# A split float32r down projection and a norm formed in the layer before it

## The reference

```python
y = depthwise7x7(x) ; y = layernorm(y) * ln_w + ln_b
y = gelu(y @ w1 + b1)                              # 192 -> 768 channels
gx = sqrt(sum(y**2, axis=(1, 2), keepdims=True))   # per image and channel
nx = gx / (mean(gx, axis=-1, keepdims=True) + 1e-6)
y = grn_gamma * (y * nx) + grn_beta + y
out = x + (y @ w2 + b2)                            # 768 -> 192 channels
```

## Time and profile before

| | |
|---|---|
| median of 3 runs (lowest to highest) | 3556.2 us (3555.02 to 3557.4) |
| the profiled execution: its own time | 3558.36 us |
| its span, first to last instruction | 3556.6 us |
| mean granted TensorE clock | 0.979 |
| TensorE, VectorE, ScalarE, GpSimd busy | 96%, 67%, 50%, 30% |
| down projection, first to last product | 2793.96 to 3178.3 us |
| the norm's block | 2779.1 to 2790.9 us |

### The profile page before, as it was taken

How to read it: one execution, slowest core, us unless ns; L and a number is a source line. 1 busy time by engine, 2 the same in 40 slices (tenths; PEclk the granted TensorE clock), 3 DMA queues, 4 the chain that set the end, 5 groups by cost and what they waited for, 6 DMA issues and landing times. The chain is left out here.

```text
span 3556.6 us, 85540 instructions
## 1 busy us (share of the span) xinstructions
PE 3410.2 (96%) x31678; PEld 3290.8 (93%) x31678; DVE 2395.2 (67%) x5939; ACT 1795.4 (50%) x5312; POOL 1052.3 (30%) x1951
## 2 busy tenths in 40 slices
PE   7999999999799999999988869999999899999999
PEld 6888888888699999999978869989999899999999
DVE  5777777777556767767679979979999311125554
ACT  5666666666444444444446656669999100002222
POOL 4333333333244444444423310014444232320000
PEclk9999999999899999999999989999999899999999
DMA  1455566610011111111168765537777788877775
GB/s 37 133 193 195 198 238 235 234 57 24 26 34 49 52 51 51 51 51 51 51 187 248 243 197 189 197 125 197 197 197 197 228 254 252 254 234 229 224 229 173
DMA packets 472784, 556.39 MB, mean 156 GB/s; under 512 B 78259, under 2 KB 331958, under 8 KB 472374
## 3 DMA queue, kind: packets, MB, share of 16 engines
q1 hardware_dynamic: 447030, 531.65, 48.7%
q10 hardware_dynamic: 25344, 19.27, 1.7%
HBM read 392.56 MB, written 271.52 MB: 187 GB/s over the span
## 5 line engine op out<-in xcount | busy, mean ns | idle before, releaser
L1441 PE MATMUL PS<-dw_grid,dw_mats 128*128 128x196 f32 (+1 forms) x3840 | 625.9, 327 | 33.8 <-DVE dw_mats L1373 33.8
L1441 PEld LDWEIGHTS PS<-dw_grid,dw_mats 128*128 128x128 f32 x3840 | 625.1, 192 | 34.3 <-issue 34.3
L1408 ACT ACTIVATE dw_res<-PS,dw_brow 128x196 f32<-128x196 f32 x192 | 81.7, 425 | 696.3 <-PE PS L1441 696.3
L1256 PE MATMUL PS<-mlp_w,mlp_hid 128*128 128x192 f32 x2352 | 414.4, 326 | 0.5 <-ACT mlp_hid L813 0.5
L1369 DVE COPY dw_grid<-X 32x392 f32<-32x392 f32 (+1 forms) x480 | 290.2, 605 | 163.2 <-PE PS L1441 148.9
L1668 PEld LDWEIGHTS PS<-gain,down_hid 128*128 128x128 f32 x2352 | 384.1, 191 | 4.2 <-DMA down_hid<-scratch_hid 4.2
L1668 PE MATMUL PS<-gain,down_hid 128*128 128x192 f32 x2352 | 384.4, 327 | 3.7 <-DMA down_hid<-scratch_hid 3.7
L1256 PEld LDWEIGHTS PS<-mlp_w,mlp_hid 128*128 128x128 f32 x2352 | 378.6, 190 | 0.8 <-ACT mlp_hid L813 0.8
L813 ACT ACTIVATE mlp_hid<-PS,mlp_b 128x256 f32<-128x256 f32 x588 | 247.1, 472 | 112.1 <-PE PS L804 112.0
L1656 DVE TENSOR_TENSOR X<-PS,down_x 128x192 f32<-128x192 f32 x196 | 70.2, 358 | 318.0 <-PE PS L1668 313.2
L813 ACT ACTIVATE hid_hid<-PS,hidw_b 128x256 f32<-128x256 f32 x588 | 240.8, 471 | 38.1 <-PE PS L804 38.1
(11 more groups left out here) (228 smaller groups left out, 9308.4 us busy)
## 6 DMA issues: line engine op xcount, KB each, us to landing
scratch_hid<-hid_hid SPq DMA_DIRECT2D x196, 384.0 KB, 3.8
down_hid<-scratch_hid SPq DMA_DIRECT2D x196, 384.0 KB, 4.0
scratch_wide<-scratch_taps SPq DMA_DIRECT2D x64, 960.0 KB
dw_raw<-scratch_wide SPq DMA_DIRECT2D x96, 640.0 KB, 4.3
scratch_wide<-scratch_taps SPq DMA_DIRECT2D x64, 768.0 KB
dw_raw<-scratch_wide SPq DMA_DIRECT2D x96, 512.0 KB, 3.3
scratch_u<-mlp_u SPq DMA_DIRECT2D x56, 378.0 KB, 3.0
att_x<-in_x SPq DMA_DIRECT2D x196, 96.0 KB, 1.9
```

Source lines behind the costliest of these rows:

```text
L1256: last = nc.tensor.matmul(psD[i], hid[:, p.buf(2), m, i * 128:(i + 1) * 128], w2[:, m, :], start=(m == 0), stop=(m == MC - 1))
L1441: last = nc.tensor.matmul(dst[:, :, ys, :], m, src, start=(i == 0), stop=(i == len(steps) - 1))
```

## The change

In the down projection each hidden value is split as in the up layer: ScalarE writes the high part (`hi`, a ring of three), VectorE subtracts it from the value and writes the low part over the value itself (`hid` and `low` lie at one place, seven buffers). The gain is split too, high and low beside each other. For each of the six groups TensorE multiplies the high part by both gains (384 columns, into two halves of a bank) and the low part by the high gain (192 columns, into the first half). The constant row is no longer added by GpSimd but is a 13th product, of 33 rows, with the row's high part in row 0 and its low part in row 32. VectorE then adds x2 to the first half and the second half to that, two additions, the second of which depends on the first. The x2 ring has four buffers instead of seven, and its load waits for the first addition (`part`).

The sixth hidden group no longer goes through HBM: the up layer writes it into columns 0 to 127 of X for that block, whose old contents are no longer needed; its low part (subtraction on GpSimd) is written in its place. Stores and loads of hidden values shrink from 384 to 320 KB.

`response_norm` is gone. Its loads, sums, mean and gain for the first image and the constant row are placed in steps of the up layer (the root at step 54, `form` in the steps from 58 on, one small instruction each); the second image's gain is formed in the first steps of the down projection.

```diff
+            g.load(sp)
...
-                    nc.gpsimd.tensor_copy(at(ss, p.n), part[:, p.buf(2), :]).then_inc(q["ss"], 1)
+                    g.collect(pool, p, part[:, p.buf(2), :])
...
+                if t.n == g.FIRST - 4:
+                    g.root(pool, 0)
...
+                if t.n >= g.FIRST:
+                    g.form(dve, 0, t.n - g.FIRST)
...
+                if t.n == 12:
+                    g.constant(pe)
+                if t.n == g.FIRST - 2:
+                    g.sums(pe, 0)
```

Of `Gains`, the class that holds the norm now, the methods that the steps call:

```diff
+    def constant(self, pe):
+        pe.wait_ge(self.q["beta"], 2)
+        for m in range(MC):
+            last = self.nc.tensor.matmul(self.psC, self.beta[:, m, :], self.w2[:, m, :], start=(m == 0), stop=(m == MC - 1))
+        last.then_inc(self.q["const"], 1)
...
+    def root(self, pool, img):
+        pool.wait_ge(self.q["ss"], (img + 1) * (NP // IMG))
+        self.nc.gpsimd.tensor_tensor(self.gx[:, img, :], self.tot[:, img, :], self.phalf[:, :], ALU.pow).then_inc(self.q["gx"], 1)
...
+        if 5 <= k < 5 + MC:
+            m = k - 5
+            dve.wait_ge(q["scaled"], img * 2 + 2)
+            nc.vector.tensor_scalar(gain[:, m, 0, :], self.w2[:, m, :], scale[:, m:m + 1], None, ALU.mult).then_inc(q["gain_high"], 1)
+        if 5 + MC <= k < 5 + 2 * MC:
+            m = k - 5 - MC
+            dve.wait_ge(q["gain_high"], img * MC + m + 1)
+            nc.vector.scalar_tensor_tensor(gain[:, m, 1, :], self.w2[:, m, :], scale[:, m:m + 1], as_f32(gain[:, m, 0, :]),
+                                           ALU.mult, ALU.subtract).then_inc(q["gain"], 1)
```

The new down projection, engine by engine:

```diff
+    R, XR, HR, BANKS, LAG = 7, 4, 3, 7, 2
...
+                if b.reached(R):
+                    sp.wait_ge(q["down"], b.n - R + 1)
+                sp.dma_start(hid[:, b.buf(R)], d["hid"][b.n]).then_inc(hloaded[b.buf(R)], 16)
+                if b.reached(XR):
+                    sp.wait_ge(q["part"], b.n - XR + 1)
+                sp.dma_start(x2[:, b.buf(XR), :], d["x2"][b.n]).then_inc(xloaded[b.buf(XR)], 16)
...
+                pool.wait_ge(q["high"], b.n + 1)
+                nc.gpsimd.tensor_tensor(X_low[b.n][:, :], kept(b), as_f32(hi[:, b.buf(HR), KEPT, :]), ALU.subtract).then_inc(q["low_kept"], 1)
...
+                act.wait_ge(hloaded[b.buf(R)], b.turn(R) * 16 + 16)
+                if b.reached(HR):
+                    act.wait_ge(q["down"], b.n - HR + 1)
+                nc.scalar.activation(hi[:, b.buf(HR), KEPT, :], kept(b), ACT.Identity)
+                nc.scalar.activation(hi[:, b.buf(HR), 0:KEPT, :], hid[:, b.buf(R)], ACT.Identity).then_inc(q["high"], 1)
...
+                b = t
+                if b.inside(NB):
+                    dve.wait_ge(q["high"], b.n + 1)
+                    nc.vector.tensor_tensor(low[:, b.buf(R)], hid[:, b.buf(R)], as_f32(hi[:, b.buf(HR), 0:KEPT, :]), ALU.subtract).then_inc(q["low"], 1)
+                b = t.back(LAG)
+                if b.inside(NB):
+                    dve.wait_ge(xloaded[b.buf(XR)], b.turn(XR) * 16 + 16)
+                    dve.wait_ge(q["down"], b.n + 1)
+                    nc.vector.tensor_tensor(part[:, b.buf(2), :], ps(b, 0), x2[:, b.buf(XR), :], ALU.add).then_inc(q["part"], 1)
+                    dve.wait_ge(q["part"], b.n + 1)
+                    nc.vector.tensor_tensor(X[:, b.n, :], ps(b, 1), part[:, b.buf(2), :], ALU.add).then_inc(q["out"], 1)
+                if t.n >= FIRST:
+                    g.form(dve, 1, t.n - FIRST)
...
+                pe.wait_ge(q["low"], b.n + 1)
+                pe.wait_ge(q["low_kept"], b.n + 1)
...
+                for m in range(MC):
+                    rest = low[:, b.buf(R), m, :] if m < KEPT else X_low[b.n][:, :]
+                    nc.tensor.matmul(both, hi[:, b.buf(HR), m, :], g.gain[img][:, m, :, :].rearrange("p e c -> p (e c)"), start=(m == 0), stop=False)
+                    last = nc.tensor.matmul(ps(b, 0), rest, g.gain[img][:, m, 0, :], start=False, stop=False)
+                last = nc.tensor.matmul(ps(b, 0), g.ones_r[:, :], g.row_r[:, :], start=False, stop=True)
+                last.then_inc(q["down"], 1)
```

More of the change, by code:

```diff
@@ L805, in up, with gelu @@
             last.then_inc(q["up"], 1)
-    def gelu(self, act, pair, hid):
+    def gelu(self, act, pair, place):
         nc, q = self.nc, self.q
@@ L1448, in hidden @@
+def hidden(nc, a, d, X, PS, w1, g, stack):
     s = Scope(nc, "hid", stack)
@@ L1457, in hidden, with place, two @@
     BY_ACT = 2
+    def place(p, m):
+        return hid[:, p.buf(HR), m, :] if m < KEPT else X[:, bass.ds(p.n * 2, 2), 0:128]
+    def two(m):
+        ap = squares[:, m, :]
+        return ap if m < KEPT else ap.rearrange("p (b t) -> p b t", b=2)
     with nc.Block() as block:
@@ L1624, in project, with ps, kept @@
[L1624 to L1631, removed]
+def project(nc, a, d, X, X_low, PS, g, base):
+    s = Placed(nc, "down", base, DOWN_PLAN)
+    R, XR, HR, BANKS, LAG = 7, 4, 3, 7, 2
+    FIRST = 6
+    KEPT = MC - 1
+    hi = s.sb("hi", [128, HR, MC, 128], F32R)
+    hid = s.sb("hid", [128, R, KEPT, 128])
+    low = s.sb("low", [128, R, KEPT, 128], F32R)
+    x2 = s.sb("x2", [128, XR, C])
+    part = s.sb("part", [128, 2, C])
+    hloaded, xloaded = s.sems("hloaded", R), s.sems("xloaded", XR)
+    q = {x: s.sem(x) for x in ("high", "low", "low_kept", "down", "part", "out")}
+    def ps(b, half):
+        return PS[:, b.buf(BANKS), half * C:half * C + C]
+    def kept(b):
+        return X[:, b.n, 0:128]
@@ L1659, in _ @@
+            unrolled(NB, LAG, body)
         @block.tensor
         def _(pe):
-            for img in range(IMG):
-                def body(b):
-                    b = Step(b.g, b.j + img * PER, R)
-                    pe.wait_ge(hloaded[b.buf(R)], b.turn(R) * 16 + 16)
-                    if b.reached(R):
-                        pe.wait_ge(q["out"], b.n - R + 1)
-                    for m in range(MC):
-                        last = nc.tensor.matmul(PS[:, b.buf(R), 0:C], hid[:, b.buf(R), m, :], gain2[:, img, m, :], start=(m == 0), stop=(m == MC - 1))
-                    last.then_inc(q["down"], 1)
-                unrolled(PER, 0, body)
+            pe.wait_ge(g.q["row_ready"], 1)
@@ L1673, in build @@
+            unrolled(NB, 0, body)
 def build(nc, a, out):
```

152 lines of the change are left out of this document (122 added, 30 removed).

## The result

The changed kernel takes 3586.5 us (median of 4 runs, 3583.1 to 3587.6) against 3555.6 (4 runs, 3552.7 to 3557.4) on the same chip: ratio 1.0087, 95% interval 1.0075 to 1.0099, 31 us slower. The forecast said slower, with 3564 in a range of 3531 to 3590: the direction and the range hold, the size doesn't (8 us forecast, 31 measured), and the mechanism that was to decide, a loop through the loads, did not: TensorE did. That 31 us still lie in the range is luck: its upper end was there for a late landing of the loads, which didn't come.

What follows compares the result with a forecast made beforehand. TensorE bounds the down projection now, at 1.961 us a block; afterwards a loop at 2.037 would. 196 blocks take 399.2 against 384.4, +14.8; start -7.2, end +0.4: +8.0, so 3564 us, range 3531 to 3590.

Steps and rivals of the forecast that it cites:

- a loop through the loads: Down projection: part, x2 load, hidden load, high, low form a closed loop advancing three blocks; 2.037 us a block.
- TensorE per block: Down projection: six float32r products of 384 columns and seven of 192 sum to 1.79 us a block.
- 7 x 0.11: Down projection: six products of 192 columns and the bias product at 0.11 us each on TensorE.
- wrong if the TensorE row in that stage stays full: Sign against the forecast in the down projection, tied to rival 1 with spacing 1.8 to 1.85; forecast had TensorE idle some 10%.
- rival 1: Down projection: landing is short, 2.8 us, and the loop hides at 1.84 a block; 3526 us, chance 0.20.
- rival 2: Down projection: hidden load's landing stays at 3.8 us, period 2.17, +34, 3590 us; chance 0.14.
- fixed part: The down projection loop's terms without the landing of the hidden load: 2.71 us.
- the forecast's 3.3: Down projection: landing of the 320 KB hidden load, taken as 3.3 us between bounds of 2.8 and 3.8.
- Rival 3: Down projection: GpSimd goes before VectorE's low in nearly every block; period 2.147, +29.6, 3586 us; chance 0.13.
- the 0.1 a block: Down projection: GpSimd's low part goes first in one block of four, making VectorE's low 0.43 us late; 0.1.
- The start: First down product 7.2 us earlier: first load at 2781.9, after 2.8 us added to the up layer, product 4.85 later.
- The sum: Whole kernel: down projection +14.8 us, start -7.2, end +0.4, in all +8.0.

Runs made afterwards that it cites:

- e6: Changed kernel with seven x2 buffers instead of four, the 33-row bias product kept; 3590.0 us.
- e3: Changed kernel with the bias product on 128 rows instead of 33 and seven x2 buffers instead of four; 3521.6 us.
- e7: Changed kernel without the bias product (output lacks the constant row) and with seven x2 buffers instead of four; 3500.0 us.
- e8: Changed kernel with the bias product on 64 rows instead of 33, four x2 buffers; 3592.2 us.
- e9: Changed kernel with the bias product on 128 rows, four x2 buffers, and block b's hidden load issued before block b-2's x2 load; 3521.0 us.
- e1: Changed kernel without the 33-row bias product (output lacks the constant row); 3569.1 us.
- e2: Changed kernel with the bias product on 128 rows instead of 33, added rows zero, four x2 buffers; 3567.4 us.
- e5: Changed kernel with three x2 buffers instead of four, the 33-row bias product kept; 3725.0 us.
- e11: Kernel before with gain2, cvec and ss at the high end of free SBUF, so the up layer's tiles begin 12.3 KB a partition lower; 3543.5 us, one run.
- e12: Kernel before with the sixth hidden group kept in X and the tiles moved as in e11; 3549.0 us, one run.
- e4: Changed kernel with the down projection in float32 again: no split, one addition, seven x2 buffers, constant row left out; 3545.5 us.
- e10: Kernel before with only the sixth hidden group kept in X, so hidden stores and loads are 320 KB; 3555.9 us.

## Why the forecast was right in direction and wrong in size

**The bias, and TensorE per block.** The step that failed is the term "7 x 0.11" of TensorE per block: one of those seven is the 33-row product. Six pairs at 0.285 are 1.71, where the forecast had 6 x 0.28 = 1.68; that this fits is partly luck, 0.20 + 0.09 where 0.17 + 0.11 was taken. The seventh product adds 0.455, in the steady 2.165 (e6 and the changed kernel), and not 0.11; e3, e7 and e8 show that this is 0.345 for the unlike row count and 0.11 for the product. TensorE therefore sets 2.165, above the loop's 2.04, and the condition "wrong if the TensorE row in that stage stays full" came true, not with rival 1's 1.84 but with 2.18, which is rival 2's period without its cause: the landing was 3.1 and not 3.8.

The Trainium skill (TensorE: Matmul & The Clock Gate, Part 3, The mechanism) says that a weight load is pulled ahead of running products where it goes to other row groups, or to the background buffer. Here 128-row loads behind 128-row products, the same rows, start 0.09 to 0.17 ahead of their own products, and it is the 33-row load and the 128-row one behind it that aren't pulled ahead: the trace bears out the second clause at most. The same page (Why this matters for your kernels) has a single product of 32 rows take the time of one of 128; between 128-row products, one of 33 or 64 rows costs 0.345 us more here (32 wasn't run), and the measurement decides.

The trace of before held this price. The Sobel stage has runs of four 33-row products among 128-row float32 ones. Its weight loads in the kernel before, a stretch of the timeline:

```profile
2000.67 0.64 PEld L1034 LDWEIGHTS PS<-sobel_bias_r,sobel_ones_r 33*128 33x128 f32 x4 [0.23 <-issue]
2001.47 0.79 PEld L1037 LDWEIGHTS PS<-sobel_wf,sobel_edge 128*128 128x128 f32 x5 [0.16 <-issue]
```

The idle time "issue" ahead of the first 33-row load and ahead of the first 128-row load behind them marks the loss, 0.23 and 0.16 us. The same stretch shows that what costs is the change in the row count, not fewer rows: behind one another the four 33-row loads (x4) follow without a gap, 0.64 us in all. The four products, three of 384 columns and one of 192, take 0.81 us to the start of the next 128-row one:

```profile
2000.67 0.88 PE L1034 MATMUL PS<-sobel_bias_r,sobel_ones_r 33*128 33x384 f32 x4
2001.48 0.43 PE L1037 MATMUL PS<-sobel_wf,sobel_edge 128*128 128x192 f32 x1
```

Four uncovered ones, at the 0.28 from the 33-row product to the next in the changed kernel, would take 1.12. The forecast took the pitch from two neighbours of 128 rows, where a row with the right shape stood elsewhere.

**The loop.** Its terms were nearly right (fixed part 2.5 to 2.6 instead of 2.71), and so was its cause (e9). It decides in e1, e2 and e5, and is hidden in the changed kernel (e6). The landing is 3.1 in the changed kernel and 3.7 in e1 and e2: the forecast's 3.3 lies between. With 3.7 the loop alone gives (2.60 + 3.7) / 3 = 2.10, 412 us for the stage instead of the 399 forecast. That is e2, the kernel that the forecast had in mind, and it is 10 us slower than before, near the +8.0, because a stage 12 us longer and a start 6 us earlier than forecast partly cancel. So the direction isn't luck alone: with a bias product at 0.11 the change would have been slower too, by the loop.

The fit that rival 1 takes from the Trainium skill (DMA: Bandwidth & Descriptors, Anatomy of one DMA) is given there for transfers that GpSimd issues, and these are SyncE's: its estimate of 2.75 lies under every kernel's median at 320 KB, 3.0 to 3.8.

**Rival 3, GpSimd first.** It fell. The low parts over 640 columns take 0.824 to 0.827 us in every block of 2900 to 3100, never more; GpSimd's subtraction takes 1.09, where two thirds of the earlier trace rows's 0.591 would be 0.4 or so. GpSimd is the one that waits, and in the changed kernel off the path. Its group in that stretch, duration as least, median, most:

```profile
L1746 POOL TENSOR_TENSOR X_low<-X,down_hi x92: 1092/1094/1105, 2901.0 to 3098.8; 128x128 fp32r<-128x128 f32 x92
```

The same view of VectorE's subtraction:

```profile
L1765 DVE TENSOR_TENSOR down_low<-down_hid,down_hi x92: 824/826/827, 2900.9 to 3098.7; 128x640 fp32r<-128x640 f32 x92
```

VectorE's low starts first, and GpSimd ends some 0.3 behind its end. The other order exists as well. In 26 of e2's 196 blocks VectorE is still in an addition when the high parts are ready, as rival 3 has it; GpSimd then takes 0.45 to 0.48, and low is the late one. One such block of e2:

```profile
2931.45 0.47 POOL L1746 TENSOR_TENSOR X_low<-X,down_hi 128x128 fp32r<-128x128 f32 x1 [1.20 <-ACT down_hi L1756]
...
2931.51 1.09 DVE L1765 TENSOR_TENSOR down_low<-down_hid,down_hi 128x640 fp32r<-128x640 f32 x1
```

The Trainium skill (SBUF — State Buffer, Who interferes with whom) has a VectorE instruction with two SBUF inputs and a GpSimd instruction that reads SBUF exclude each other, and the order of issue decide who blocks; both orders here agree. The forecast's mechanism was right and its size too large: of the 0.1 a block nothing is left in the changed kernel (no such block in 196) and 0.01 in e2.

**The start.** Forecast 7.2 us earlier, measured 13.5. The first hidden load goes out at 2772.95 and the first product follows 5.1 later (forecast 4.85):

```profile
2772.95 0.37 SPq L1734 DMA_DIRECT2D down_hid<-scratch_hid  x1
...
2775.81 0.31 ACT L1755 ACTIVATE down_hi<-X 128x128 fp32r<-128x128 f32 x1 [6.32 <-DMA down_hid<-scratch_hid]
...
2776.78 0.83 DVE L1765 TENSOR_TENSOR down_low<-down_hid,down_hi 128x640 fp32r<-128x640 f32 x1 [6.72 <-ACT down_hi L1756]
```

The rest is the up layer. Its tiles' new place gives 9.5 us (402.6 in the mean of e11 and e12, one run each, against 412.1), which no term of the forecast had. The norm's steps in it cost 408.4 - 402.6 = 5.8, twice the 2.8 forecast: the stretches with the `form` steps have 855 and 849 products for 864. So 9.5 - 3.0 - 0.25 = 6.25 more than forecast, which is the difference of 6.3. The norm's move itself is worth 13.5 - 9.5 = 4 us.

**The sum.** Forecast +8.0. Down projection 427.9 instead of 399.2, +28.7; start -6.3; end +0.5; together +30.9, as the medians have it (+30.9).

## What to carry to other kernels

Price an added instruction by a row with its own shape, however far from the edit that row stands, and by the starts of its neighbours: a product with another row count than those around it cost three times itself in weight loads that lost their cover, and padding it to 128 rows won back 65 us once the loads kept up. Where two loads share a queue, follow what each waits for: a small load that waits for a recent result holds back the large one behind it, and issuing it two blocks later (e9) did as much as three more buffers (e3). When several limits lie close together, as here 2.165, 2.10 and 1.82, removing the first shows only the distance to the second (e2), and only both together show the gain.

## What the runs showed of the hardware that was not expected

- Among 128-row float32r products, one of 33 or of 64 rows costs 0.455 us of TensorE, one of 128 rows 0.11: neither its weight load nor the next one is hidden. Behind one another 33-row products keep the cover (0.81 us for four in the Sobel stage).
- Float32r products of 384 and 192 columns that alternate take 0.20 and 0.09 from start to start, 0.285 a pair; at the 0.11 of the earlier trace rows for 192 columns the pair would have been 0.31.
- Where tiles lie in SBUF changes TensorE's rate in the up layer by 2.2% (845 and 864 products in 100 us at full clock, e11), with nothing else changed.
- The landing of a 320 KB load was 3.0 to 3.3 us at the median in the kernels that moved 152 to 197 GB/s between 2900 and 3100 us (the changed one, e5, e6, e8) and 3.6 to 3.8 in those that moved 203 to 251 (e1 to e4, e7, e9, e10, e12), whether TensorE or the loads set the pace. The DMA share doesn't part them: 0.71 in e8 (3.3) and in e2 (3.7). Why stays open.
- VectorE's subtraction over 640 columns takes 0.83 us when it starts first and up to 1.12 when GpSimd's starts first; GpSimd's over 128 takes 1.09 and 0.46 in the same two cases.
